# Adding the four weighted expert pairs on the Pool engine before TensorE turns them back

## The reference

```
logits = xf @ gate_w + gate_b
top2_vals, top2_idx = top_k(softmax(logits), 2)
cw = zeros(N, 8).at[tokens, top2_idx].add(top2_vals)
for e in range(8):
    h = gelu(xf @ W1[e] + b1[e])
    out += cw[:, e] * (h @ W2[e] + b2[e])
```

## Time and profile before

| | |
|---|---|
| median of 3 runs | 1323.69 us (1318.94 to 1325.88) |
| the profiled execution, its own time | 1326.46 us |
| its span, first to last instruction | 1325.0 us |
| TensorE busy | 1082.3 us, 82% of the span |
| VectorE busy | 650.9 us, 49% |
| ScalarE busy | 480.9 us, 36% |
| Pool engine busy | 450.2 us, 34% |
| mean granted clock of TensorE | 0.851 of full speed |
| `turn_back` of the 24 expert blocks (L1382) | 768 matmul rows, 91.1 us busy |

### The profile page before, as it was taken

How to read it: one execution, slowest core, us unless ns; L and a number is a source line. 1 busy time by engine, 2 the same in 40 slices (tenths; PEclk the granted TensorE clock), 3 DMA queues, 4 the chain that set the end, 5 groups by cost and what they waited for, 6 DMA issues and landing times.

```text
span 1325.0 us, 18705 instructions
## 1 busy us (share of the span) xinstructions
PE 1082.3 (82%) x5362; PEld 687.9 (52%) x5362; DVE 650.9 (49%) x2388; ACT 480.9 (36%) x903; POOL 450.2 (34%) x1306
## 2 busy tenths in 40 slices
PE   3555378786998989988499998979999676999998
PEld 2444366663554545544345557766666343445544
DVE  3665675553554454553355544454554554454441
ACT  0222111124544344543245543223443111565564
POOL 4444535551234433344633311114555211010100
PEclk9999999556878788787679995557999886999999
DMA  4400000000000000000000000000000000000000
GB/s 69 73 0 0 1 0 0 0 1 0 1 0 1 0 0 0 0 1 1 1 1 0 0 1 0 0 1 1 0 0 1 0 0 0 5 4 4 8 4 9
DMA packets 26263, 6.31 MB, mean 5 GB/s; under 512 B 23974, under 2 KB 26150, under 8 KB 26214
## 3 DMA queue, kind: packets, MB, share of 16 engines
q1 hardware_dynamic: 26214, 5.72, 2.4%
HBM read 4.66 MB, written 1.05 MB: 4 GB/s over the span
## 4 chain that ended last, share of the span: by engine, by line
PE 52%; issue 11%; DVE 5%; POOL 5%; ACT 3%; ACTq 0%; DVEq 0%; POOLq 0%
PE banks L1357 8%; PE banks L1189 6%; PE banks L1382 5%; PE banks L1080 4%; PE banks L1011 3%; PE banks L1479 3%; PE banks L1081 3%; POOL ex L644 2%; PE banks L1374 2%; PE banks L1467 2%; PE banks L1181 2%; PE banks L1443 2%; PE banks L1177 1%; PE banks L1165 1%; PE banks L1144 1%
## 5 line engine op out<-in xcount | busy, mean ns | idle before, releaser
L635 POOL TENSOR_TENSOR rstd<-vareps,neghalf 128x4 f32<-128x4 f32 x64 | 67.2, 1049 | 324.4 <-DVE vareps L1603 317.3
L893 ACT ACTIVATE scratch<-banks,b 128x512 f32<-128x512 f32 x224 | 144.1, 684 | 67.3 <-PE banks L1081 62.6
L1357 PE MATMUL banks<-scratch,W 128*64 128x512 f32 (+1 forms) x448 | 148.1, 654 | 0.0
L1876 DVE SCALAR_TENSOR_TENSOR weighted<-banks,b,cwide 128x512 f32<-128x512 f32 x96 | 71.9, 749 | 146.4 <-PE banks L1357 144.5
L1771 DVE TENSOR_TENSOR scratch<-banks,XR 128x1024 f32<-128x1024 f32 x72 | 87.5, 1224 | 113.8 <-PE banks L1181 86.3
L1080 PE MATMUL banks<-VS,W_hi 128*128 128x512 f32 x240 | 118.0, 492 | 2.2 <-DVE X L1933 1.0
L1054 PE MATMUL banks<-ident,V 128*128 128x128 f32 x128 | 34.4, 361 | 94.0 <-DVE V L1614 90.9
L693 ACT ACTIVATE VS<-banks 64x256 fp32r<-64x256 f32 x112 | 42.4, 379 | 187.9 <-PE banks L1054 180.3
L904 ACT ACTIVATE cwide<-banks 128x512 f32<-128x512 f32 x96 | 57.4, 598 | 129.6 <-PE banks L1374 129.4
L1081 PE MATMUL banks<-VS,W_lo 128*128 128x512 f32 x240 | 103.1, 430 | 0.0
L1189 PE MATMUL banks<-scratch,region 128*64 128x256 f32 x576 | 96.9, 467 | 3.0 <-DVE scratch L1771 3.0
(11 more groups left out here) (273 smaller groups left out, 2145.7 us busy)
## 6 DMA issues: line engine op xcount, KB each, us to landing
X<-in_x SPq DMA_DIRECT2D x8, 128.0 KB, 2.7
region<-in_L_ffn_W SPq DMA_DIRECT2D x2, 512.0 KB
out<-X SPq DMA_DIRECT2D x8, 128.0 KB, 2.0
W<-in_L_ffn_W SPq DMA_DIRECT2D x1, 512.0 KB
region<-in_L_ffn_W SPq DMA_DIRECT2D x2, 256.0 KB
scratch<-in_L_conv_kernel SPq DMA_DIRECT2D x2, 144.0 KB
W<-in_L_ffn_W SPq DMA_DIRECT2D x1, 256.0 KB
region<-in_L_ffn_w SPq DMA_DIRECT2D x2, 128.0 KB
```

The costliest lines, as they stand in the source:

```text
L635: pool.tensor_tensor(rstd[:], vareps[:], neghalf[:], ALU.pow).then_inc(rstd_ready, 1)
L893: act.activation(hid[:, c % 4, :], bank[c % 2][:, :], ACT.Gelu, bias=b1[s][:, w:w + 1]).then_inc(h_ready, 1)
L1357: ins = pe.matmul(y, W2[s][:, w, :], hid[:, c % 4, :], start=opens, stop=closes, skip_group_check=True)
L1876: vec.scalar_tensor_tensor(weighted[:, u, j, :], bank[2 + j % 2][:, :], b2[s][:, j:j + 1], cwide[:, j, :], ALU.add, ALU.mult).then_inc(pai ...
```

## The change

The Pool engine adds the four pairs as a tree, pair 0 + pair 1, pair 2 + pair 3, and the sum of both, and TensorE turns back only that sum: 4 matmuls in place of 16. `summed` is a new tile of two 128 x 512 buffers, `sum_ready` a new semaphore. Core of the diff:

```diff
+        summed = sb("summed", [P, 2, BLK])
...
+            def sum_pairs(i, s, u):
+
+                p = i * (2 * PAIRS) + (PAIR0[s] + u * PAIRS + PAIR_CREDIT)
+                m = i * 2 + (MOE0[s] + u)
+                for h in range(2):
+                    pool.wait_ge(pair_used, p + 2 * (h + 1))
+                    if h == 0:
+                        pool.wait_ge(out_psum, m + 1)
+                    link(pool.tensor_tensor(summed[:, h], weighted[:, u, 2 * h, :], weighted[:, u, 2 * h + 1, :], ALU.add))
+                pool.tensor_tensor(summed[:, 0], summed[:, 0], summed[:, 1], ALU.add).then_inc(sum_ready, 1)
...
                     if first_half:
                         seg2(step)
+                    if s in MOE:
+                        sum_pairs(i, s, u)
                     if s not in (0, 1) and second_half:
                         seg3(step)
                     if second_half:
                         if not (s == 5 and wrap):
                             front()
+                        rewind()
+                    elif s in (3, 7):
                         rewind()
...
                 if s == 6:
                     sigma()
+                    rewind()
...
+            pe.sem_inc(out_psum, 1)
...
-            def turn_back(b, p, s, u):
-
-                pe.wait_ge(pair_used, p + (PAIRS + PAIR_CREDIT))
+            def turn_back(b, m, s, u):
+
+                pe.wait_ge(sum_ready, m + 1)
                 pe.wait_ge(block_done, b + (NB * s + CREDIT))
                 for t in range(NT):
-                    for j in range(PAIRS):
-                        ins = pe.matmul(bank[5][:, t * C:(t + 1) * C], weighted[:, u, j, t * P:(t + 1) * P], fold[:],
-                                        start=(j == 0), stop=(j == PAIRS - 1))
+                    ins = pe.matmul(bank[5][:, t * C:(t + 1) * C], summed[:, 0, t * P:(t + 1) * P], fold[:],
+                                    start=True, stop=True)
                 ins.then_inc(out_psum, 1)
...
-                    vec.wait_ge(out_psum, m + 1)
+                    vec.wait_ge(out_psum, m + 2)
```

More of the change, by code:

```diff
@@ L297, in metaformer @@
         out_psum = sem("out_psum")
+        sum_ready = sem("sum_ready")
         om_ready = sem("om_ready")
@@ L1433, in expert_stage @@
                         turn_cw(m + 1, p + PAIRS, 1 - u)
-                    turn_back(b, p, s, u)
+                    turn_back(b, m, s, u)
             def attention_products(u):
```

## The result

The changed kernel takes 1444.83 us (median of 4 runs, 1442.27 to 1446.36) against 1321.32 us for the kernel before beside it: ratio 1.0935 [1.0885, 1.0986], 9% slower. The forecast was 1370 us in a range of 1340 to 1402. The direction was right; the time lies 43 us above the range. (The ratios leave out executions more than 1.5% above the fastest of the same kernel; the medians given with them don't.)

The account below looks back on a forecast made before the run. TensorE was taken as the bound from block to block, with turn_back on its path. Terms -1.4 + 13.2 + 7.0 + 5.3 + 22 = +46 us on 1326.5 gave 1372.6, less 2.8 for the median: 1370 us, range 1340 to 1402.

Parts of the forecast that it names:

- Removed: TensorE's turn at each block's end: eight rows in place of 32 take 2.72 us off each of 24 blocks, 65.3 us.
- The adds: Two Pool adds between weight 3 and the turn, 1.25 us each: 2.66 us more TensorE idle time per block.
- The rival of cheap adds: Pool adds take 0.62 us each and the clock holds: 1307 us, chance 0.04.
- `seg3` and `front` behind the adds: Stage 5: seg3 starts after the last add, so TensorE waits 4.4 us before slot1 at three places, 13.2 us.
- The adds behind `seg2`: Stage 5, first blocks: all three adds follow seg2, delaying the turn; 2.3 us in three blocks, 7.0 us.
- Stage 6: End of stage 5: the last seg3 starts behind the last add, so rstd of stage 6 comes 5.3 us later, uncovered.
- The clock: Low-clock stretches behind half of 21 block boundaries in stages 3, 5, 7 and three stage 5 stalls: 22 us.
- the chain of stage 5: Stage 5's Pool work moved behind other work: 13.2 us for seg3 behind the adds, 7.0 us for adds behind seg2.
- The low clock that lasts: Rival: stage 3 low throughout, 48 us, and 12 us for half of 14 other boundaries: 1408 us, chance 0.12.
- The held clock: Rival: the granted clock does not fall and the rest of the sum stays: 1348 us, chance 0.20.
- The Pool engine does hold up VectorE: Rival: VectorE's two-input operations wait for the Pool add; weight 3 1.25 us later in 11 blocks: 1384 us, chance 0.10.

Follow-up runs that it names:

- e8: Kernel before, but TensorE turns back pair 3 alone: 4 matmuls in place of 16, no Pool add, no new wait, output differs; single run 1286.66 us.
- e1: Changed kernel plus 20 unused matmuls on constants (fillers) on TensorE in its wait for the sum, in all 24 expert blocks; 1373.69 us, ratio 1.0395.
- e6: Changed kernel's Pool engine with its adds, but TensorE turns back all four pairs as before and nobody waits for the sum; 1368.15 us, ratio 1.0301.
- e2: Changed kernel, but stage 5 adds and turns back as before the change; the Pool engine's sums stay in stages 3 and 7; 1408.82 us, ratio 1.066.
- e5: Changed kernel with its adds and wait for the sum, but TensorE turns back all four weighted pairs, 16 matmuls, sum unused; 1585.33 us, ratio 1.1887.
- e4: Against the kernel before, Pool adds pairs 0 to 2 early and TensorE turns back that sum and pair 3, in all three stages; 1329.8 us, ratio 1.0053.
- e10: As e1, plus in first blocks of stage 5's pairs 40 fillers ahead of slot1 and 40 for 20 in the sum wait; 1370.08 us, ratio 1.0368.

## Why the prediction was right or wrong

**Removed: right.** Eight rows take 1.10 to 1.11 us at full clock (forecast 1.07) and 1.97 us at the low one, and where nothing waits the shorter turn is worth 2.7 to 2.9 us a block (e8, stages 3 and 7).

**The adds: right.** 1.26 us each against 1.25; TensorE's wait is 2.82 to 2.85 us in most blocks of stages 3 and 7, against some 2.7. (In stage 5 it is 2.33 to 5.59 us.) With 256 columns an add takes 0.72 us, so the slope of two inputs is about 2.1 ns a column. The rival of cheap adds is out. The Trainium skill's figure (GPSIMD Engine Reference, section 3.1), from which an estimated 1.12 us had been worked out, lies 11% under the measured 1.26 us.

**`seg3` and `front` behind the adds: right in size, but overtaken.** In e1 the wait before `slot1` is 4.5 us. In the changed kernel it is 0.93 us, timeline of its stage 5:

```profile
969.07 0.58 PE L1044 MATMUL banks<-ones 64*128 64x1 f32 x2 [0.93 <-POOLq L609]
```

TensorE is itself so late by then that the rest of the wait is hidden behind slow matmuls. A sum of separate terms counts such a wait and the slow clock twice. In e6 the wait is nothing, and stage 5 loses 31.0 us all the same, at the low clock.

**The adds behind `seg2`: right.** Stage 5 of the changed kernel:

```profile
985.23 0.20 POOL L488 TENSOR_TENSOR nsq<-nsq,sq 128x2 f32<-128x2 f32 x1
...
985.67 1.26 POOL L659 TENSOR_TENSOR summed<-weighted 128x512 f32<-128x512 f32 x1 [0.24 <-POOL nsq L488]
987.09 1.26 POOL L659 TENSOR_TENSOR summed<-weighted 128x512 f32<-128x512 f32 x1 [0.16 <-POOL summed L659]
988.43 1.26 POOL L660 TENSOR_TENSOR summed<-summed 128x512 f32<-128x512 f32 x1
```

All three follow `seg2`'s last instruction, and the sum is there 4.3 us after it (forecast 4.05). It happened in every first block, the first pair's too, which had been put at nothing. What it costs in time (7.0 us by the forecast) no run shows by itself.

**Stage 6: right.** 4.7 us against 5.3; rstd starts right behind `seg3`, and e2 takes it away.

**The clock: this step failed.** The place was right (the stop lowers the clock, shown by e5, and fillers in it bring it back, e1), but "I take it that half of them are followed by one such stretch ... 22 us" was a guess at how often and for how long it stays low, from one stretch of 3.3 us. In the changed kernel a low stretch follows every stop of stages 3 and 7, of 6.8 to 20.5 us but for one of 3.4 us ahead of the last block of stage 7, with full clock in between; stage 5 has one of 78.5 us. In time: stage 3 goes from 162.6 us (e1) to 195.7, 33 us, and stage 7 from 215.2 to 242.8, 28 us. These 61 us are measured. For stage 5 no run shows the length at the old clock: against e1, itself at 0.71, the loss is 12 us, and against the 171.1 us that the prediction's terms give (150.9 + 13.2 + 7.0) it is 36 us. So the term is 73 to 97 us in place of 22. Taken at 97, with what e1 leaves in stages 3 and 7 (6.4 + 0.2), 20.2 for the chain of stage 5, stage 6 (4.7), stage 4 (1.9) and the 10.3 us less in stages 1 and 2, the sum is the 119.9 us of the spans; but that it closes is no evidence, since the 36 us are what was left over. (If the 5.7 us of VectorE's wait, which stage 3 of the changed kernel doesn't show, are taken from e1's stage 3, the clock's share is 6 us larger.) The prediction had the price of one low block (6.9 us). What it had wrong is their number and length: one short stretch behind half of the boundaries, where in fact nearly every boundary had a longer one.

**The rivals.** The low clock that lasts came nearest, with a chance of 0.12 and a price of 1408 us that was 37 us too low, since it put the lasting low clock in stage 3 only; the range stopped at 1402. The held clock, 1348 us, is 26 us under e1's 1373.69 us. Of these 6 us are VectorE's wait, and most of the rest lies in stage 5 (194.9 us against 171.1); how much of that is its low clock isn't shown. The Pool engine does hold up VectorE: an operation of 128x32 took 0.18 us alone and 1.14 us beside a Pool add (e1, e6), 5.7 us of TensorE's time in stage 3, and up to 2.22 us a block in e4. In stage 3 of the changed kernel it doesn't happen, because the add and that operation don't meet (L1875 has a mean of 181 ns); in its stage 5 three rows of the normalization (L1632, 1.27 us for 0.31) and in its stage 7 six of L1879 (0.66 for 0.17) are held. These have one input tile, so it isn't only operations of two inputs; the weighting of 128x512 (L1894), which reads the bank, keeps its 0.75 us. By the lock on a shared port pair that the Trainium skill states (SBUF — State Buffer, section "two separate sides") it should be so, and here the traces agree, but for one thing: beside the exponential of 5.43 us, also an operation of two inputs on the Pool engine, VectorE's rows of two inputs kept their 0.19 us in the kernel before. Timeline of its stage 3, to be read with the exponential at 687.03 in the earlier trace rows:

```profile
688.26 0.19 DVE L1847 TENSOR_TENSOR oh<-l,m 128x32 f32<-128x32 f32 x1
688.48 0.19 DVE L1848 TENSOR_TENSOR sc<-oh,prio 128x32 f32<-128x32 f32 x1
```

**What stays open.** Why stage 7 recovers with a stop of 1.77 us and stages 3 and 5 don't; what lowers the clock of stage 5 in e6 and e8, where nothing stops TensorE ahead of the turn; why the stretch behind `slot1` stays low longer in e10 than before; and why a full turn behind the stop (e5) leaves the clock lower (0.56) than a short one (0.66).

## What to carry to other kernels

When TensorE is the bound and its clock is above its low level, an idle gap put into each round costs its own length and then the clock of the rounds behind it: here 24 gaps, most of 2.8 us and nearly paid for by removed work, cost at least the 71 us more that fillers gave back. Price such a change at both clock levels for whole stages and let the range reach the low one; keep a helper engine's work where it ends before the last operand does (adding three pairs early and turning two in stage 7 gave 1.3%), and first look at what stands behind the moved work on the helper's queue, and at what VectorE does beside it (in stage 3 of e4 the same adds made TensorE wait 2.22 us for VectorE). If a gap can't be avoided, try fillers in it: 20 matmuls on constants gave back 71 us.

## What the runs showed of the hardware

- A busy TensorE was faster than one with less to do: e1 executes 480 matmul rows more than the changed kernel (5266 against 4786) and takes 71 us less.
- In stages 3 and 7 a turn of a quarter of the matmuls with no stop kept the clock (0.86, 0.95). In stage 5 it did not in the one execution profiled (0.67 from 0.86).
- VectorE's operations on 128x32 and 128x64 floats wait out a Pool add of 128x512 (1.14 us for 0.18, 1.27 us for 0.31), but its weighting of 128x512 doesn't (0.75 us), and none waits out the Pool engine's exponential of 5.43 us.
- The clock fell where TensorE had waited 2.8 us for the sum (stage 3 of the changed kernel), 2.22 us for `cw` (e4) and 1.34 us for `cw` (stage 5 of e6), and not where it waited 0.83 us (stage 5 of the kernel before). Behind waits of 1.2 to 1.3 us in stage 3 of e1 and e6 it fell once, in e6.
